# A gated cross-attention with eight experts: a scatter pair, early and late tables, the ninth tile's transposition and the clearing of the tails are moved

## The reference, cut to what matters

```
xn   = layernorm(x)
att  = xn @ w_input.T + (xn * dot_scale) @ ctx.T - 1e30 * mask
x    = x + tanh(g_xattn) * softmax(att) @ ctx
h    = layernorm(x)
p    = softmax(h @ W_router.T);  gates, e = top_k(p, 2);  gates /= sum(gates)
y    = sum over the two experts of gate * W_down[e] @ (silu(W_gate[e] @ h) * (W_up[e] @ h))
out  = x + tanh(g_ffn) * y
```

## Time and profile before

| what | value |
|---|---|
| runs, us | 257.2, 257.57, 260.07 (median 257.57) |
| profiled execution, its own time | 254.09 us |
| its span from first to last instruction | 252.3 us |
| PE, PEld busy | 222.3 us (88%), 175.7 us (70%) |
| DVE, ACT, POOL busy | 137.9 us (55%), 116.1 us (46%), 112.7 us (45%) |
| mean granted PE clock | 0.97 of full speed |
| DMA | 44.38 MB, mean 176 GB/s |

### The profile page before, as it was taken

How to read it: one execution, slowest core, us unless ns; L and a number is a source line. 1 busy time by engine, 2 the same in 40 slices (tenths; PEclk the granted TensorE clock), 3 DMA queues, 4 the chain that set the end, 5 groups by cost and what they waited for, 6 DMA issues and landing times.

```text
span 252.3 us, 5442 instructions
## 1 busy us (share of the span) xinstructions
PE 222.3 (88%) x1431; PEld 175.7 (70%) x1432; DVE 137.9 (55%) x499; ACT 116.1 (46%) x270; POOL 112.7 (45%) x197
## 2 busy tenths in 40 slices
PE   7799999999999999988799899799999999999100
PEld 6377767786676867667488688688888888887000
DVE  4566556868778678676965366333344334332043
ACT  3173434563455645555474345345555454454000
POOL 3455331568645585456356755344432333333300
PEclk9999999999999999999999999999999999999855
DMA  6999999999879977958634501321211110000284
GB/s 184 322 404 270 359 270 314 306 303 260 304 277 250 353 249 221 274 173 263 246 83 141 183 19 40 84 66 64 55 42 45 52 43 31 21 21 34 60 221 130
DMA packets 19771, 44.38 MB, mean 176 GB/s; under 512 B 3690, under 2 KB 10134, under 8 KB 19734
## 3 DMA queue, kind: packets, MB, share of 16 engines
q1 hardware_dynamic: 16396, 39.26, 50.3%
q0 software_dynamic: 2560, 3.77, 4.6%
q10 hardware_dynamic: 790, 1.04, 1.6%
HBM read 37.71 MB, written 6.34 MB: 175 GB/s over the span
## 4 chain that ended last, share of the span: by engine, by line
PE 67%; DMA 8%; DVE 8%; issue 7%; POOL 6%; SPq 1%; ACT 1%; DVEq 0%; ACTq 0%; POOLq 0%
PE psum L1129 15%; PE psum L1232 11%; PE psum L1101 9%; PE psum L1205 6%; PE psum L1206 5%; PE psum L1207 5%; PE psum L1216 5%; PE psum L1118 4%; DMA ctxT<-in_ctx_cols 3%; DMA ctx_sb<-results 3%; POOL pair_rows L554 2%; PE psum L1091 2%; PE psum L1191 1%; POOL var L508 1%; PE psum L1137 1%
## 5 line engine op out<-in xcount | busy, mean ns | idle before, releaser
L642 POOL DMA_INDIRECT results<-y_sb,dest x32 | 30.7, 959 | 52.2 <-DVE dest L1011 26.0
L1129 PE MATMUL psum<-ctx_sb,probsT 128*100 128x128 f32 (+1 forms) x384 | 52.6, 281 | 0.0
L1129 PEld LDWEIGHTS psum<-ctx_sb,probsT 128*100 128x100 f32 (+1 forms) x384 | 43.8, 166 | 3.2 <-issue 0.2
L1022 DVE SCALAR_TENSOR_TENSOR scores<-probs,row_in,psum 128x512 f32<-128x512 f32 x32 | 23.9, 748 | 38.8 <-ACT probs L732 32.1
L1101 PE MATMUL psum<-ctxT,qT 128*100 128x512 f32 (+1 forms) x96 | 41.8, 571 | 1.1 <-DMA ctxT<-in_ctx_cols 1.1
L667 ACT ACTIVATE probsT<-psum 128x400 f32<-128x400 f32 x48 | 20.7, 505 | 42.0 <-PE psum L1118 41.9
L586 POOL DMA_INDIRECT slots<-pair_rows,slot_i x32 | 33.5, 1046 | 12.9 <-issue 6.3
L732 ACT ACTIVATE probs<-psum 128x512 f32<-128x512 f32 x32 | 19.1, 597 | 35.5 <-PE psum L1207 34.4
L1232 PE MATMUL psum<-w_down,hidT 128*128 x256 | 34.2, 276 | 0.4 <-issue 0.4
L1232 PEld LDWEIGHTS psum<-w_down,hidT 128*128 128x128 f32 x256 | 31.1, 192 | 0.8 <-issue 0.8
L1205 PE MATMUL psum<-w_hi,rowT_hi 128*128 x64 | 28.4, 443 | 1.7 <-issue 1.0
(11 more groups left out here) (136 smaller groups left out, 304.3 us busy)
## 6 DMA issues: line engine op xcount, KB each, us to landing
ctxT<-in_ctx_cols SPq DMA_DIRECT2D x16, 722.0 KB, 8.6
ctx_sb<-in_ctx SPq DMA_DIRECT2D x16, 704.0 KB
w_raw<-in_w_experts SPq DMA_DIRECT2D x16, 256.0 KB
maskb<-mask_scaled SPq DMA_DIRECT2D x5, 541.5 KB
row_in<-slots SPq DMA_DIRECT2D x32, 65.0 KB
w_down<-in_w_experts SPq DMA_DIRECT2D x4, 512.0 KB
slots<-empty SPq DMA_DIRECT2D x8, 195.0 KB
ctx_sb<-results SPq DMA_DIRECT2D x4, 192.0 KB, 5.5
```

The source lines that it names most:

```text
L642: nc.gpsimd.indirect_dma_start(results, bass.IndirectOffsetOnAxis(ap=dest[:, s:s + 1], axis=0), y_sb[:, s, :], None).then_inc(y_stored[s], 16)
L1022: nc.vector.scalar_tensor_tensor(out=hidden[k % 2], in0=silu[k % 2], scalar=row_in[:, o, D:D + 1], in1=up_ps[k % 2], op0=ALU.mult, op1=ALU ...
L1129: last = nc.tensor.matmul(attn_ps[0:Q, 0:D], probsT[0:rows[c], c, :], ctx_sb[0:rows[c], b % CTX_RING, c, :], start=(c == 0), stop=(c == CH ...
```

## The change

Seven edits of the order in which work is issued; no operation of the computation is added or taken away.

- POOL: `scatter(11)` and one wait for landed late scatters move from behind `normalise2` of batch 14 to before `root2` of batch 14, directly behind `scatter(10)`, with the wait ahead of the scatter. The two waits for landed late scatters that stood before `scatter(12)` and `scatter(13)` are gone.
- DVE: `tile_rows(False)` moves from the end of step 14 into step 15, behind `statistics2(13)`.
- DVE: the splitting of weight chunk 14 (`split_weights`) moves in step 15 from before to behind `masked_max(15)` and `tile_experts(False)`.
- DVE: `tile_runs(True)` runs after tile step 3, `tile_rows(True)` after 4, `tile_experts(True)` after 5, each one step sooner.
- PE, ACT, DVE: the rows of tile 9 are transposed, rounded and split at the end of step 8, as those of tile 8 are at the end of step 7, and no longer at the beginning of step 8.
- PE: `ranks(LAST)` stands in step 3 before the transposition of tile 2's hidden block, no longer behind it.
- SP: the eight clearing transfers are issued behind the load with n = 4 (`YRING // 2`), which is the fifth, no longer behind the eighth.

```diff
@@ SP @@
                 load_rows(0, n)
-                if n == EARLY - 1:
+                if n == YRING // 2:
                     sp.wait_ge(tails_ready, 1)
                     for e in range(E):
                         clear_tail(e)
@@ POOL @@
                 if 5 <= b:
                     scatter(b - 5)
+                if b == B - 1:
+                    pair_landed(1)
+                    scatter(11)
...
             root2(B - 2)
             normalise2(B - 2)
-            scatter(11)
-            pair_landed(1)
             scatter(12)
             root2(B - 1)
             normalise2(B - 1)
-            pair_landed(1)
             scatter(13)
             last_gates()
@@ ACT, DVE and PE tile_step; rowT_high, rowT_low and transpose_rows alike @@
-                if 0 < k and k + 1 < T and k != EARLY - 1:
+                if 0 < k and k + 1 < T and k not in (EARLY - 1, EARLY):
                     transpose_rows(i, k + 1)
...
-                if k == EARLY - 1:
+                if k in (EARLY - 1, EARLY):
                     transpose_rows(i, k + 1)
@@ DVE step @@
                     residual(b - 2)
                     statistics2(b - 2)
+                if b == B - 1:
+                    tile_rows(False)
                 if b >= 1:
                     attention_gain(b - 1)
                 split = ROUNDED.get(b - 1, ())
-                for c in split[:1]:
-                    split_weights(c)
+                if b < B - 1:
+                    for c in split[:1]:
+                        split_weights(c)
                 masked_max(b)
...
                     tile_experts(False)
-                    for c in split[1:]:
+                    for c in split:
                         split_weights(c)
...
-                if b == 14:
-                    tile_rows(False)
@@ DVE between @@
                 if n == 3:
                     tile_counts(True)
+                    tile_runs(True)
                 if n == 4:
-                    tile_runs(True)
+                    tile_rows(True)
                 if n == 5:
-                    tile_rows(True)
-                if n == 6:
                     tile_experts(True)
@@ PE tile_step @@
                 if k == 2:
                     transpose_xn2(B - 1)
+                if k == 3:
+                    ranks(LAST)
                 if 0 <= k - 1 < T:
                     transpose_hidden(i, k - 1)
...
-                if k == 3:
-                    ranks(LAST)
                 if k - 2 >= 0:
                     down(i, k - 2, e)
```

## The result

| | before | changed |
|---|---|---|
| median of six runs each, us | 256.98 (254.86 to 260.07) | 252.67 (252.16 to 254.87) |
| profiled execution, its own time; span | 254.09; 252.3 | 252.16; 250.3 |

The ratio is 0.9864, 95% interval [0.9815, 0.9914]: faster by 1.4%, where 257.5 us and no change were forecast, and the time lies under the range. The two profiled executions differ by 1.9 us only, the medians by 4.3, so more than half of the gain is not between the two traces that the prediction compared. On three other chips the ratio was 0.9992 (no gain), 0.9904 and 0.9875; over all sets the mean of 35 executions of the changed kernel is 253.9 us, that of 128 of before 256.8.

The account below looks back on a forecast made before the run. PE was taken as the bound, full from tile step 9, so only gate_up(9)'s start mattered: -0.55 - 0.77 + 0 + 0 + 1.3 = 0.0 us, hence 254.1 us for the execution and 257.5 us median, range 254.8 to 260.0.

Parts of the forecast that it names:

- The prediction's own sign against it: On PE, gate_up(9) starting under 162 us would show the forecast wrong; it was expected near 162.9.
- Step 1, early table: DVE's early table moved: PE resumes 1.0 us sooner at batch 13, shrinking to 0.55 us at the first gate_up.
- Step 2, scatter 11 ahead: POOL's scatter 11 before batch 14: PE's 0.77 us hole before batch 15's rows goes, the new wait staying hidden.
- Rival C: POOL's new wait between scatters 10 and 11 delays batches 14 and 15: +2.1 us, 259.7 us; chance 0.10.
- D: Row 5's load, behind the clears, comes late for PE: a few tenths to 1 us, 258.5 at most; chance 0.05.
- Step 3, ranks: PE's ranks(LAST) ahead of a transposition: same matmuls in another place of the step, cost 0.
- Step 5, ninth rows late: On PE, tile 8's transposition to gate_up(9): one stall becomes two, 6.33 us against 5.05, +1.3 us.
- Step 4, the late chain: Late tables sooner, tails cleared behind the fifth load: load 8 leaves earlier, yet value 0, bounds 0 and -0.15 us.
- Rival A: Tile 8's start hangs only on landed scatters, so both stalls around tiles 8 and 9 go: -3.5 us, 254.1; chance 0.06.
- The step from the execution to the median: The profiled execution ran 3.5 us below before's median; the same gap was assumed for the changed kernel, giving 257.5 us.

Follow-up runs that it names:

- no_ninth2: The changed kernel with the ninth tile's rows transposed early again, in their old place; run in two sets: 252.64 us (ratio 0.9845) and 252.54 us (0.9867).
- again: The kernel before, unchanged, run and profiled once more: 257.52 us, ratio 1.0021 to before.
- warm_before: The kernel before with 11 idle PE matmuls around tile 8's late transposition: 256.87 us, ratio 1.0059 to before.
- delay1: The changed kernel with one idle POOL operation ahead of scatter 14: 253.46 us, ratio 0.9895 to before.
- no_clear: The changed kernel with the tails cleared behind the eighth load, as before: 253.78 us, ratio 0.9876 to before.
- delay2: The changed kernel with two idle POOL operations ahead of scatter 14: 256.89 us, ratio 1.0039 to before.
- code_before: The kernel before with 32 more PE instructions at the start (2 idle matmuls out, 10 tiny ones in): 258.71 us, ratio 1.0026 to before.
- no_pool: The changed kernel with POOL's old order of scatters 11 to 13: 256.32 us, ratio 0.9981 to before.
- only_ninth: The kernel before with only the ninth tile's rows transposed late: 257.08 us, ratio 1.0044 to before.

## Why the prediction was wrong

The median was forecast 4.8 us too high, in two parts. Between the profiled executions the sum was 0.0 and their times differ by -1.9; and 3.4 us were added from the execution to the median, where the changed kernel's median lay only 0.5 us above its profiled execution. The prediction's own sign against it came true: `gate_up(9)` at 161.55, under 162. In spans (-2.0 us), the parts are these:

- **Step 1, early table.** The sign and the mechanism were right, the size too small. The prediction let 0.4 us of the hole before batch 13 stay; nothing stayed, PE was there 1.85 us sooner, of which 0.37 us is a lead that the attention already had at 116 us. DVE had no idle time from 120.46 to 127.79, as forecast, and `residual(14)` stood at 127.79 against 128.3. Before the first `gate_up` the gain shrank to 1.07 us (129.57 for 130.64), or 0.7 without that lead, where 0.55 was forecast; PE's idle time there grew by 0.14 + 0.42 us, where 0.45 was forecast.
- **Step 2, scatter 11 ahead.** Right: scatter 11 at 128.54 (forecast from 128.7), batch 14's rows at 132.58 (133.3 or later), batch 15's at 137.13 (138.0) and no hole. From batch 13's transposition to tile 8's the stage is 32.03 us against 32.41, -0.4 where steps 1 and 2 gave +0.45 - 0.77 = -0.3. Rival C did not occur; D neither: row 5, whose load was issued behind the clears from 139.94 on, was transposed at 143.73 without idle time of PE.
- **Step 3, ranks.** Nothing in these traces speaks against 0; it was not tried alone.
- **Step 5, ninth rows late.** Right in sign and form, two stalls of 0.84 with 0.60 of issue behind: 5.96 us, where 6.33 was forecast, +0.9 instead of +1.3. no_ninth2 gives +1.0 in time, the intervals overlapping.
- **The rest** of the two traces: 0.1 us more behind `gate_up(9)`, and 0.8 us less behind the last transposition of rows (26.62 against 27.44), in the tail and the final loads, which no edit touches.
- **Step 4, the late chain, is the step that failed**: "Taking the transfer away alone gains nothing. Value 0, bounds 0 and -0.15." For the shown execution this holds, and load 8 went out at 152.98 (153.5 was forecast), 2.6 us ahead of its use for 2.0 before. But before's trace had escaped a collision by 0.2 us: the scatter's data were through at 150.25 us and the block of code started at 150.47. again, one further profile of the same kernel, had the collision, 1.4 us of waiting for row 8 and the fall of the clock. Of the 128 executions of before 81 had a mean granted clock under 0.967, with a median of 257.8 us, and the other 47 one of 254.9; of the changed kernel 9 of 35 (256.1 and 253.3). So some 1.6 us of the gain are alike at equal clock, and some 1.0 us more come from the clock falling in 26% of the executions and no longer in 63%. How much of either is the late chain's is argued, not shown: falls stood at the start (warm_before, delay1) and around the first tile (no_ninth, no_clear, delay1) as well. What is shown is that the collision, put back into the changed kernel, takes its whole gain (delay2). Rival A (the late chain was the bound, 0.06) was nearest in mechanism, though for the wrong execution and without the price of the clock.
- **The step from the execution to the median** failed with it. I carried 3.5 us over to the changed kernel ("That execution ran 3.5 us below the median ... the changed kernel's median I therefore put at 257.5 us"). These 3.5 us did not carry over. A part of them was the cost of the late chain, which an edit can remove, and which the single trace did not contain; another was slower starts (0.8 us in again), and falls of the clock elsewhere may have added to it. The shares were not measured.

What the profile would have allowed: load 8 was issued at 155.83, 2.0 us ahead of its use, and PEld waited for row 9 to 159.10, 0.1 us past the split of tile 8; a chain without cover in an execution below the lowest of the runs shown may well be exposed in the others.

**Open.** What share of the executions has the collision was not counted, since only profiled ones show it; it was there in four of the five further profiles of kernels with before's late tables, code_before being the fifth. Which of the late tables, the ranks and the early table frees the scatter was not tried alone; no_pool and no_clear kept the short wait without POOL's order and without the moved clears, in one profiled execution each, and no_pool was no faster than before all the same. Why PE's clock fell in some executions with such a hole and not in others (1.36 + 0.78 us in only_ninth and 0.99 + 0.58 in the shown before without a fall, 1.51 + 0.78 in delay2 and 0.86 + 0.53 in code_before with one) is also open.

**Best version.** two_buf, the change without the late ninth rows and with a second buffer: 251.23 and 252.18 us in its two sets, ratios 0.9836 [0.9790, 0.9883] and 0.9774 [0.9702, 0.9846] to before, and under the changed kernel on both chips (255.36 and 253.19), clear of noise on the first only. What the second buffer adds to no_ninth was not tried on one chip: the traces give 0.9 us (3.97 for 4.90, and 4.18 in two_buf2), the ratios of no_ninth (0.9845 and 0.9867) overlap those of two_buf.

## What to carry to other kernels

When the profiled execution is faster than every run shown, don't carry the difference over as a constant: look for the wait in it that had the least cover, and price what comes if that cover is gone. A transfer chain that lands within a tenth of a microsecond of its use can be the bound in other executions, and a hole of PE that it opens can cost more afterwards through the clock than by itself (2.5 us for 1.4 in again). Where one late transposition must wait for one buffer, give the next a second buffer before moving it.

## What the runs showed of the hardware

- A block of PE's code is one packet of 0.02 MB that took 1.2 to 1.3 us (before, again, delay2). Started 1.7 us behind a scatter's issue it delayed the scatter's last three packets by 0.9 us and the waiting POOL by 1.6 us (delay2 against delay1), as it did in again; 2.2 us behind the issue (the shown before) it cost nothing.
- At half clock one tile step took 5.34 us instead of 2.86 (again). A mean clock of 0.967 or more was kept by 47 of 128 executions of before, 26 of 35 of the changed kernel, 11 of 12 of only_ninth and 4 of 10 of delay2. Holes of PE of like length were followed by the fall in some executions and not in others.
- Behind a transposition that had waited, `gate_up` started only after a further 0.45 to 0.60 us charged to issue (0.58 before, 0.60 in the changed kernel, 0.45 in again, 0.53 in code_before); idle matmuls in that place did not shorten the run.
